# Cross-attention and FP4 feed-forward: six x tiles quantized ahead in batches 6 to 12, the weight shares of the last batch moved to batches 12 to 14

## The reference

```
x = x + attention(layernorm(x), ctx, ctx)       # 16 heads of 32, softmax over 750 keys
x = x + ffn(layernorm(x))
fp4(v):     blocks of 16: scale = max(max|v| / 6, 1e-12); v / scale rounded to the
            grid 0, .5, 1, 1.5, 2, 3, 4, 6 with its sign, times scale
linear(a, w) = fp4(a) @ fp4(w).T
ffn(a) = linear(silu(linear(a, w_gate)) * linear(a, w_up), w_down)    # 512 -> 1408 -> 512
```

## Time and profile before

| | |
|---|---|
| three runs | 2137.6, 2138.82, 2141.08 us; median 2138.82 |
| the profiled execution | 2137.12 us, of which the span is 2135.3 us |
| busy over the span | PE 2070.8 us (97%), DVE 1708.5 (80%), ACT 863.6 (40%), POOL 144.7 (7%) |
| mean granted clock of TensorE | 0.987 |
| DMA | 257.36 MB, mean 121 GB/s |

### The profile page before, as it was taken

How to read it: one execution, slowest core, us unless ns; L and a number is a source line. 1 busy time by engine, 2 the same in 40 slices (tenths; PEclk the granted TensorE clock), 3 DMA queues, 4 the chain that set the end, 5 groups by cost and what they waited for, 6 DMA issues and landing times. The chain is left out here.

```text
span 2135.3 us, 42263 instructions
## 1 busy us (share of the span) xinstructions
PE 2070.8 (97%) x16730; PEld 1785.7 (84%) x16730; DVE 1708.5 (80%) x2859; ACT 863.6 (40%) x1753; POOL 144.7 (7%) x162
## 2 busy tenths in 40 slices
PE   6999999999999999999999999978899999999998
PEld 5888888888988888888888898856688888888886
DVE  6777777777777777777768777777999999999985
ACT  5555455455554555555545455453111111111111
POOL 0000000000000000000000000001101001001000
PEclk9999999999999999999999999979899999999999
DMA  4443444534445344344553545454343343344331
GB/s 162 119 137 98 130 110 135 140 97 132 109 133 139 101 126 139 100 137 109 132 139 95 132 109 134 111 151 129 107 133 109 113 137 112 114 131 113 114 113 38
DMA packets 159462, 257.36 MB, mean 121 GB/s; under 512 B 34096, under 2 KB 102704, under 8 KB 156832
## 3 DMA queue, kind: packets, MB, share of 16 engines
q1 hardware_dynamic: 158544, 253.34, 43.1%
q10 hardware_dynamic: 720, 1.31, 0.2%
HBM read 109.88 MB, written 57.54 MB: 78 GB/s over the span
## 5 line engine op out<-in xcount | busy, mean ns | idle before, releaser
L756 DVE TENSOR_REDUCE row_max<-gate_bank 128x1 f32<-128x376 f32 (+1 forms) x576 | 301.8, 536 | 114.6 <-PE gate_bank L565 113.6
L539 PE MATMUL proj_bank<-attention_operands 128*128 128x256 f32 x2304 | 304.8, 282 | 0.0
L517 PE MATMUL proj_bank<-attention_operands 128*128 128x376 f32 (+1 forms) x1536 | 288.8, 337 | 3.6 <-ACT attention_operands L690 3.1
L539 PEld LDWEIGHTS proj_bank<-attention_operands 128*128 128x128 f32 x2304 | 288.8, 189 | 0.4 <-DVE q_part L786 0.2
L654 ACT ACTIVATE probs<-score_bank 125x448 f32<-125x448 f32 x384 | 208.0, 542 | 163.5 <-PE score_bank L579 161.1
L517 PEld LDWEIGHTS proj_bank<-attention_operands 128*128 128x128 f32 x1536 | 262.1, 190 | 5.9 <-issue 3.4
L1402 ACT ACTIVATE f_act_gate<-gate_bank 128x512 f32<-128x512 f32 (+1 forms) x84 | 47.3, 564 | 528.4 <-PE up_bank L1342 528.4
L654 ACT ACTIVATE probs<-up_bank 125x448 f32<-125x448 f32 x384 | 208.0, 542 | 126.7 <-PE up_bank L579 124.2
L1342 PE MATMUL gate_bank<-gate_up,early 128*128 128x512 f32 (+1 forms) x984 | 226.7, 380 | 17.2 <-DVE early L1484 9.3
L1342 PEld LDWEIGHTS gate_bank<-gate_up,early 128*128 128x128 f32 x984 | 183.7, 191 | 50.2 <-DVE early L1484 9.6
L1342 PE MATMUL up_bank<-gate_up,early 128*128 128x512 f32 (+1 forms) x984 | 223.8, 376 | 0.0
(11 more groups left out here) (146 smaller groups left out, 3194.5 us busy)
## 6 DMA issues: line engine op xcount, KB each, us to landing
kstack<-k_low SPq DMA_DIRECT2D x256, 93.8 KB, 2.3
kstack<-early SPq DMA_DIRECT2D x256, 93.8 KB, 2.2
kstack<-k_high SPq DMA_DIRECT2D x256, 93.8 KB, 2.2
strips_scratch<-f_strips SPq DMA_DIRECT2D x25, 960.0 KB, 3.7
f_turned<-strips_scratch SPq DMA_DIRECT2D x100, 240.0 KB, 4.4
ctx_raw<-in_ctx SPq DMA_DIRECT2D x15, 1500.0 KB, 8.0
qstack<-early SPq DMA_DIRECT2D x384, 28.0 KB, 1.9
qstack<-q_part SPq DMA_DIRECT2D x384, 28.0 KB, 1.8
```

Of the source, the lines that this page charges most:

```text
L517: last = nc.tensor.matmul(out[:, 0:hi - lo], w_hi_lo[W_K][ws][:, c, g * P:(g + 1) * P], ctx_part[cs][:, c, lo:hi], start=(n == 0), stop=(n ...
L539: last = nc.tensor.matmul(out[:, 0:256], ctx_part[cs][:, c, kt * KW:kt * KW + P], w_hi_lo[W_V][ws][:, c, half * 256:(half + 1) * 256], sta ...
L756: nc.vector.tensor_reduce(row_max[:, m, kh:kh + 1], mbank[:, 0:KSPLIT[kh + 1] - KSPLIT[kh]], AX.X, ALU.max).then_inc(max_reduced, 1)
```

## The change

**Six x tiles ahead.** For t = 0 to 5 tile t of x1 is loaded into `xn` in batch 6+t, slot 2, normalized there, quantized in slots 2 and 3 and in slot 0 of the next batch, transposed in squares and stored to `x_ahead[t]`, all in the units `ahead_*`. The load of the next batch's x, which shares `xn`, moves from place 2.6 to 7.0, behind `ffn_regroup`, in every batch, and waits for these stores. **Tiles 0 and 1** are loaded in the last batch, slot 0, four pieces each, already turned; their normalization, quantization and turning on TensorE are gone. **Tiles 2 to 5** are loaded into `f_turned` by `x_ahead`, again in four pieces, and quantization of x with the hidden values begins in the period of tile 4. **Shares.** Slot 2 of batches 12, 13 and 14 takes a share; the last batch has none, and stores only the last one. **Order.** In the period of tile 2 the first gate and up chunk of tile 3 stands ahead of the down product (`SHIFTED`), and the first hidden product moves forward within the quantize steps of tiles 1 to 3.

```diff
+SHIFTED = 2
+AHEAD = 6
+AHEAD_BATCH = 6
-FFN_SLOTS = (0, 1, 3)
-PROJECTIONS = ("k", "q", "v", "xt", "out", "first_turn")
+FFN_SLOTS = [(b, g) for b in range(BATCHES - 1) for g in range(4) if g != 2 or b >= BATCHES - 4]
+PROJECTIONS = ("k", "q", "v", "xt", "out")
...
-        "ffn_quant": (5.33, 7.73, 8.21, 8.66, 9.42, 9.43, 9.88, 11.15, 11.15),
+        "ffn_quant": (3.84, 4.49, 4.93, 5.92, 7.04, 7.22, 9.26, 10.46, 11.22),
...
+AHEAD_UNITS = {
+    (0, 2): [(6.2, ("ahead_load",)), (10.5, ("ahead_norm",)), (11.3, ("ahead_norm2",))],
+    (0, 3): [(0.8, ("ahead_quant", 1)), (2.3, ("ahead_quant", 2)), (2.7, ("ahead_quant", 3)), (3.8, ("ahead_quant", 4)),
+             (10.4, ("ahead_quant", 5)), (10.7, ("ahead_quant", 6)), (11.2, ("ahead_quant", 7)), (11.5, ("ahead_quant", 8))],
+    (1, 0): [(2.1, ("ahead_quant", 9)), (3.0, ("ahead_square",)), (3.5, ("ahead_store",))],
+}
...
+    share_slots = [NG * n + slot for n, slot in FFN_SLOTS]
...
+        if slot + 1 == here:
+            add(0.2, ("ffn_store", chain))
+            add(6.0, ("ffn_regroup", chain))
+        if slot - 1 == here:
+            add(0.3, ("ffn_load", chain))
...
+    for (later, slot), placed_units in AHEAD_UNITS.items():
+        tile = b - AHEAD_BATCH - later
+        if slot == g and 0 <= tile < AHEAD:
...
-        add((at["load"],) * 2, ("load_ctx", 1), ("load_x", 1))
+        add((at["load"], 7.0), ("load_ctx", 1), ("load_x", 1))
...
-    placed += [(1, 3.0 + 0.6 * i, ("first_norm", i)) for i in range(2)]
-    placed += [(1, 4.8 + 0.6 * i, ("first_norm2", i)) for i in range(2)]
-    placed += [(1, 5.6 + 0.7 * s, ("first_quant", 0, s + 1)) for s in range(QSTEPS)]
-    placed += [(2, 1.0, ("first_turn", 0)), (2, 1.3, ("first_turn_hi", 0)), (2, 1.9, ("first_turn_lo", 0))]
...
+    placed += [(2, 0.3, ("first_turn_hi", 0)), (2, 0.9, ("first_turn_lo", 0))]
+    placed += [(3, 0.1, ("first_turn_hi", 1)), (3, 0.5, ("first_turn_lo", 1))]
...
+                elif kind == "ahead_load":
+                    sp.wait_ge(made["xt"], 2 * (b + 2))
+                    sp.wait_ge(x1_stored, 32 * ((P * t + P - 1) // SQ + 1))
+                    sp.dma_start(xn_whole[:, 0, :], x1.rearrange("b s d -> (b s) d").rearrange("(n p) d -> n p d", p=P)[
+                        bass.ds(t, 1), :, :].rearrange("a p d -> (a p) d")).then_inc(ahead_loaded, 16)
...
                 elif kind == "first_load":
                     sp.wait_ge(made["xt"], 2 * batches)
+                    sp.wait_ge(ahead_stored, 16 * AHEAD)
+                    for c in range(HG):
+                        sp.dma_start(xn_whole[c * DK:(c + 1) * DK, t, :].rearrange("p (g k j) -> p g k j", g=HG, k=KC),
...
                     reached(sp, made["xt"], 2 * (b + t))
+                    reached(sp, ahead_stored, 16 * min(max(b - AHEAD_BATCH, 0), AHEAD))
                     sp.dma_start(xn[:, :, :], rows(dram["x"], b + t)).then_inc(x_loaded, 16)
...
+    with_h, with_x = tile > 0, tile + 2 >= AHEAD and left > 2
...
+    hidden_at = {0: 0, 1: 4, 2: 4, 3: 6}.get(tile, 8)
+    shifted = tile == SHIFTED
...
+    return [*([] if tile == SHIFTED + 1 else [("gate_up", n, 0)]),
...
+            *strips, *when(1, *([("x_lo", n + 1)] if tile > 0 else [])), *([("x_ahead", n + 2)] if 0 < tile < AHEAD - 2 else []),
+            *([("hidden", n, 2), ("gate_up", n + 1, 0)] if shifted else []),
+            *when(-2, *[("down", n - 2, c) for c in range(3)]), *([] if shifted else [("hidden", n, 2)]), *bounce]
...
-    units = [("load", 2), ("load", 3)] + [("late_load", k) for k in range(LATE_RAWS)]
+    units = [("x_ahead", 2)] + [("late_load", k) for k in range(LATE_RAWS)]
...
-    return units + [("norm", 2), ("normalize", 2)]
+    return units
...
+                elif kind == "x_ahead":
+                    sp.wait_ge(x_lo, tile)
+                    for c in range(HG):
+                        sp.dma_start(turned[c * DK:(c + 1) * DK, :, FC:WC, :], x_ahead[tile].rearrange(
```

More of the change, by code:

```diff
@@ L202, in slot_units @@
         add(at["sum_lo"], ("sum_lo", g - 1))
[L203 to L212, removed]
+    for chain, slot in enumerate(share_slots):
+        if slot == here:
+            add(at["ffn_quant"], *[("ffn_quant", chain, n + 1) for n in range(QSTEPS)])
+            add(at["ffn_quant"][-1] + 0.02, ("ffn_square", chain))
+        if slot + 1 == here:
[3 more added lines that the diff above has]
+            add(0.3, ("ffn_load", chain))
     if g == 1 and not first:
@@ L269, in end_tiles, with batch_units @@
     return units
-def batch_units(first, last):
-    return [u for g in range(NG) for u in slot_units(g, first, last)]
+def batch_units(b):
+    return [u for g in range(NG) for u in slot_units(g, b)]
 SPLIT_ORDER = (1, 0, 2, 3)
@@ L621, in body @@
                     last.then_inc(fs["gated"], 1)
[L622 to L627, removed]
         pe.wait_ge(consts_made, 3)
@@ L1086, in quantize_step, with period_units @@
     return dve.tensor_tensor(blocks(out), blocks(t), spread(scale), ALU.mult)
-def period_units(n, first=None, left=None):
+def period_units(tile, n, left):
+    with_h, with_x = tile > 0, tile + 2 >= AHEAD and left > 2
+    event = with_h or with_x
     def has(k):
-        return (first is None or first + k >= 0) and (left is None or k < left)
+        return tile + k >= 0 and k < left
     def quant(*steps):
-        return [("quant", n, s, has(-1), has(2)) for s in steps if has(-1) or has(2)]
+        return [("quant", n, s, with_h, with_x) for s in steps if event]
@@ new lines, in fresh @@
+    def fresh(k, *units):
+        return list(units) if tile + k >= AHEAD and k < left else []
+    strips = [("strips", n, with_h, with_x)] if event else []
+    bounce = [("bounce", n, with_h, with_x)] if event else []
+    hidden_at = {0: 0, 1: 4, 2: 4, 3: 6}.get(tile, 8)
+    shifted = tile == SHIFTED
+    def quant_and_hidden(*steps):
+        return [u for s in steps for u in quant(s) + ([("hidden", n, 0)] if s == hidden_at else [])]
+    return [*([] if tile == SHIFTED + 1 else [("gate_up", n, 0)]),
+            *([("hidden", n, 0), ("gate_up", n, 1), ("hidden", n, 1)] if hidden_at == 0 else []),
+            *quant_and_hidden(1, 2, 3, 4, 5, 6), *fresh(3, ("norm", n + 3)),
+            *quant_and_hidden(7), *when(-3, ("store", n - 3)), *when(-1, ("load_res", n - 1)), *fresh(4, ("load", n + 4)),
+            *when(-2, ("h_hi", n - 2)), *when(1, *([("x_hi", n + 1)] if tile > 0 else [])), *quant_and_hidden(8),
+            *fresh(3, ("normalize", n + 3)), *quant(9), *when(-2, ("h_lo", n - 2)),
+            *([("gate_up", n, 1), ("hidden", n, 1)] if hidden_at else []), ("gate_up", n, 2),
+            *strips, *when(1, *([("x_lo", n + 1)] if tile > 0 else [])), *([("x_ahead", n + 2)] if 0 < tile < AHEAD - 2 else []),
+            *([("hidden", n, 2), ("gate_up", n + 1, 0)] if shifted else []),
+            *when(-2, *[("down", n - 2, c) for c in range(3)]), *([] if shifted else [("hidden", n, 2)]), *bounce]
@@ L1235, in phases @@
             i, n = (0, tile) if tile < 3 else ((tile - 1) // 2, 1 + (tile - 1) % 2)
-            units = period_units(n, first=tile, left=tiles - tile)
-            if tile == 0:
-                units = [u for u in units if u[0] not in ("x_hi", "x_lo")]
+            units = period_units(tile, n, tiles - tile)
             body(i, with_late(units, late[tile]) if tile < 2 else units)
@@ L1386, in body @@
                 elif kind == "h_hi":
[L1387 removed]
+                    act.wait_ge(turned_loaded, 16 * HG * (tile + 1))
                     act.wait_ge(late_lo, LATE + FC)
@@ L1516, in cross_attention_ffn @@
     x1 = nc.dram_tensor("x1_scratch", (batches, SQ, D), F32, kind="Internal").ap()
+    x_ahead = [nc.dram_tensor(f"x_ahead{t}", (P, D), F32, kind="Internal").ap() for t in range(AHEAD)]
     ffn_raw = [dram[n] for n in ("gate", "up", "down")]
```

214 lines of the change are left out of this document (106 added, 108 removed).

## The result

The changed kernel takes **2172.72 us** (median of 4 runs, 2169.38 to 2179.76) against 2139.58 us for the kernel before in the same comparison: ratio 1.0158, 95% interval 1.0146 to 1.0171. It is slower by 33 us, where 9 us faster was forecast. The profiled execution took 2170.8 us around a span of 2169.0.

The account below looks back on a forecast made before the run. The prediction took TensorE to bound the middle of the attention and DVE the seam into the feed-forward. Its terms, -11 - 5 + 7 = -9 us, gave 2130 us against the median of 2138.8, range 2126 to 2134 at chance 0.50.

Parts of the forecast that it names:

- The x load moves behind the regroup: Every batch: the x load is issued at 676 instead of 672.2; cost taken as 0, end 13 us.
- ahead_norm in front of the shift: Middle batches, end of slot 2: normalization waits for its load and delays the shift; loss 7 us, ends 0 and 12.
- The quantize steps: Middle batches: the tile's quantize steps and transpose fall in DVE gaps; cost 0, at most 0.5 us a batch.
- Fourth shares: Batches 12 to 14: the fourth share pushes the next stack by up to 4 us; cost 0, at most 3 in all.
- The last batch: Share and x chains leave DVE, so TensorE gets back its waits on them; gain 5 us, between 2 and 8.
- The start of the feed-forward: TensorE starts earlier and DVE drops the x part; gain 11 us, with TensorE waits of 2.9, 3 and 3 left.
- waits for that low part and not for h: Feed-forward start: TensorE waits for tile 3's low part, its first chunk being ahead of the down product; resumes at 47.8 us.
- Slower: Rival: the x1 load lands late at ahead_norm in all six batches; 2139 to 2155 us, chance 0.05.
- Seam gain eaten: Rival: every batch's x load, or the stacks of batches 12 to 14, cost the seam's gain; 2135 to 2143, chance 0.13.
- the time pass 2165: Within Slower: an x1 load landing after 8.5 to 10.9 us would cost each batch 5 us or more.

Follow-up runs that it names:

- e2: Kernel before with one number changed: the x load at place 7.0, behind the regroup copies; ratio 0.9997.
- e1: Changed kernel with each x_ahead store issued ahead of the context load instead of behind it; 2151.1 us.
- e7: e1 with the x1 tile's load at place 5.0 of slot 2 instead of 6.2, normalization still in slot 2; 2146.1 us.
- e8: e7 with three weight shares in every batch, as in the kernel before; 2144.66 us.
- e9: e6 with the tile's normalization moved into DVE's idle 1.8 us at the start of slot 3; 2131.51 us.
- e10: Changed kernel without quantize steps 2 to 8 of the six tiles, step 9 a plain maximum; 2163.16 us.
- e3: Changed kernel with the tile's normalization moved from the end of slot 2 into slot 3, behind the shift; 2154.6 us.
- e5: Changed kernel with the edits of e1 and e3 together; 2143.65 us.
- e6: Changed kernel with the edits of e1, e3 and e4 together; 2136.07 us.
- e4: Changed kernel with three weight shares in all 16 batches, the last included, as in the kernel before; 2158.9 us.
- e11: e9 with the feed-forward's tile order not shifted, as in the kernel before; 2126.91 us.
- e12: Changed kernel with the feed-forward's tile order not shifted, as in the kernel before; 2162.31 us.

## Why the prediction was wrong, step by step

**The step that failed is a wait priced at nothing.** The prediction costed the x load's new place ("The x load moves behind the regroup"), by its issue 4 us later, at 0 with an end of 13, and e2 bears that out: the load itself was never late for DVE, whose only wait for it is 1.7 us at the program's start, as before. But the diff gives that load also a wait for ahead_stored, and the prediction never priced it: not what SP stands at, nor what is queued behind. SP stood there for 29.6 us in six batches. Behind it stand the low stack copies, for which DVE's k_low waits, and the shares' stores, for which fw_square and so the row maxima wait. The rows for the price were there: the x load itself, issued behind the context load, landed after 8.5 to 10.9 us. A store issued behind the same load, with a wait on its landing, had to be read against that row and not against the 3.3 us of the x1 loads; it landed after 6.7 to 8.2. e1 took 22.5 us out of the six tiles' stretch by that store's place alone.

**ahead_norm in front of the shift** (loss 7, in batches 7, 10 and 11): the mechanism is right, the size off. Slot 3 of batches 6 to 11 lost 11.5 us, inside the bounds of 0 and 12. The load's landing was taken at 3.3 us and was 3.2 to 3.9, median 3.7; the estimate of 2.6 from the Trainium skill (DMA: Bandwidth & Descriptors, Anatomy of one DMA), whose section is on DMAs that GpSimd issues while SP issues this one, lies below all six. DVE waited for the x1 load in all six batches, 16.5 us in sum, and TensorE for the shift 8.2 us in five. Batches 6, 8 and 9, taken at 0 for having no regroup there, waited as well: e7 shows that the regroup made the load late in batches 10 and 11, and SP's other issues in the rest. With everything else mended, moving the normalization from slot 2 (e8) to the gap in slot 3 (e9, whose x1 load is even issued at its later place) gives 13.2 us of median time and 12.9 us in the six tiles' stretch.

**The quantize steps at 0, at most 0.5 a batch**: e10 gives 3.2 us for all six, which fits either bound and cannot be told from nothing. With the normalization behind the shift too, slot 3 of each tile's batch was 1.1 us longer (e3, e5, e6); moving the normalization into the gap took that away with the steps left in.

**Fourth shares at 0, at most 3**: 3.5 us, all of it in slot 1 of batch 14 (4.0 longer); e4 takes 3.6 out.

**The last batch, gain 5**: -0.3 in the changed kernel, -5.4 in e11. The size was reachable, but with the shares left where they were; with them moved no version gained over 2.4. Slot 2 is 3.0 or 3.1 us shorter in every run without the two x chains. In slot 1 the changed kernel loses 1.3, where the runs with the shares in place gain 1.2 or 1.3, and the rest it loses behind slot 2. There, from 12 us behind slot 2's maxima, it is at the lower level in both windows of 6 us, the kernel before in the first alone. After, then before (clock in the third column from the end):

```profile
1476.20:1482.20 6.00, 4.17 (x36) 2.02 (x35) 2.68 (x5) 3.34 (x7) 0.00 (x0) 0.50 0.97 292
1482.20:1488.20 6.00, 5.79 (x54) 3.52 (x54) 1.74 (x1) 1.94 (x4) 2.51 (x2) 0.51 0.41 128
```

```profile
1433.50:1439.50 6.00, 3.87 (x32) 2.83 (x36) 5.93 (x14) 4.20 (x9) 0.00 (x0) 0.50 0.70 202
1439.50:1445.50 6.00, 5.59 (x88) 3.38 (x81) 5.58 (x9) 2.06 (x5) 3.16 (x2) 0.95 0.70 222
```

**The start of the feed-forward, gain 11**: 10.5. Waits of 3.04, 3.49 and 2.61 stand where 2.9, 3 and 3 were forecast, and ACT has 0.01 us between the table load and the SiLU, as in the earlier trace rows and against the 1.38 us of drain in the Trainium skill (ScalarE: Activation LUTs, What ACT_TABLE_LOAD costs). Yet the sum hid a step of the wrong sign: the reordering of tile 3, which went into it as part of the gain, costs 2.6 us, and 4.2 where the low clock follows its wait. Without it the seam gives 14.7 (e12) to 15.8 (e11), so that 10.5 lies so near to 11 is in part luck. The prediction had said that TensorE "waits for that low part and not for h" and did not ask whether the old order would have waited at all.

**The rivals.** "Slower" had the outcome's sign and a chance of 0.05, with its place at the x1 load. "Seam gain eaten" named the x load and the stacks, the right place, and took its price from the load's own landing. Neither had a wait of the queue's issuer in it. Their ranges end at 2143 and 2155, so the measured 2172.7 lies outside everything that had a chance. That "the time pass 2165" stands beside "Slower" is no hit: it was worked out for an x1 load landing after 8.5 us or more, and that load landed after 3.2 to 3.9.

## What to carry to other kernels

When a change adds a wait to an in-order DMA queue, price it like an instruction: what is awaited, what was issued just ahead of it on the same queue, and who waits for each transfer behind. Here a small store issued after a large load landed with it; issued 0.5 us ahead of it, it landed after 2.7 to 3.7 us. And when a change moves several things, test each with the others in place: here one part gave 15 us, three took it away, and a fourth, a loss of 2.6 to 4.2 us, hid inside the gain.

## What was not expected of the hardware

The same 256 KB store landed after 6.7 to 8.2 us when it was issued 0.5 us behind the 1.5 MB load, and after 2.7 to 3.7 us ahead of it, with the order of SP's queue the same otherwise. The seam's clock does not follow from the wait ahead of it: after a wait of 3.04 or 3.05 us the first twelve matmuls took 4.18 us in the changed kernel, e9 and e12, some 3.6 in e4 and e5, and 2.33 us in e3 and e11. The block's first two windows in e9, then in e11:

```profile
1467.70:1473.70 6.00, 3.27 (x10) 3.30 (x11) 1.05 (x2) 2.85 (x4) 0.00 (x0) 0.66 0.64 202
1473.70:1479.70 6.00, 6.00 (x25) 5.59 (x25) 4.44 (x8) 3.02 (x6) 0.00 (x0) 0.77 0.60 193
```

```profile
1466.00:1472.00 6.00, 3.23 (x19) 3.26 (x20) 1.44 (x3) 3.25 (x5) 0.00 (x0) 1.00 0.65 205
1472.00:1478.00 6.00, 5.82 (x27) 4.66 (x26) 5.56 (x9) 2.60 (x5) 0.00 (x0) 1.00 0.69 206
```

The attention before it and the block up to there have the same instructions in both. What decides it was not found. e12, at the lower level here and 4.2 us shorter than the changed kernel in the feed-forward all the same, and e3, at the higher level with the shifted order, show that the level and the order are two things.
